# A four-layer Flamingo block on one core: two experts gated late, a third taken natively, and GpSimd work moved

## The chip, the cores and the metric

The kernel runs on one core of one Trainium2 chip. The metric is the device time in microseconds of one execution, lower is better. Five engines run side by side, each through its own list of instructions, and meet only at semaphores: TensorE (PE in the profile, its weight load PEld), VectorE (DVE), ScalarE (ACT), GpSimd (POOL) and SyncE (SP, which issues the DMAs).

## The reference

1024 tokens (4 batches of 256) of width 128 pass four residual layers, each behind a layer norm and scaled by the tanh of a scalar. Cut to what matters here:

```
x = x + tanh(gx0) * attention(LN(x), ctx)        # softmax(q k^T) v, 64 context rows per batch
x = x + tanh(gf0) * experts(LN(x))
x = x + tanh(gx1) * linear_attention(LN(x), ctx) # 16 heads of 8, softmax of q and k within a head
x = x + tanh(gf1) * quantised_mlp(LN(x))         # w_gate, w_up, w_down at 4 bits, width 384

def experts(tokens):                             # 8 experts, hidden 256
    top 2 of logits = tokens @ router_w.T;  gate[:, e] = softmax weight of expert e, or 0
    for e in range(8):
        h = gelu(tokens @ w1[e].T)
        out += gate[:, e:e+1] * (h @ w2[e].T)
```

The gate of an expert is one number per token, so it may be applied to the hidden values before the second product, or to the product itself.

## The kernel before

The tokens stand in two halves of 512 (HALVES, four tiles of 128 tokens each). The order on each engine is written out by hand.

**Experts.** The work of an expert is four units: half h (0, 1) by hidden chunk c (0, 1), so 32 units, u = 4e + 2h + c. A unit is: the product z on TensorE in three fp32r passes (high weights by high tokens, low by high, high by low), GELU on ScalarE out of PSUM (`gelu`), the gate times it on VectorE (`gate_unit`), and the second product y into bank 2 + h. For experts 2 to 6 that product is split as well: ScalarE rounds the gated values to a high part (`high`), VectorE takes the rest (`low`), and TensorE makes three passes. Experts 0, 1 and 7 are native: one fp32 product, which the trace shows as two instructions, and no `high` or `low`. A ring of NB = 4 banks and buffers holds the units in flight, and in the steady loop TensorE does y of unit u and then z of unit u + 4.

**Gates.** For each half `logits` gives the router's products, VectorE finds the best two (`top_two`) and the gates (`gates_of`). Expert 0 isn't gated before its second product: `y_first` writes bank h, and `first_expert` multiplies by the gate row late. Expert 1's row is spread over the partitions by TensorE (`second_gate`, eight small instructions a half) and copied by ScalarE. From expert 2 on the rows go through DRAM: `gate_columns` transposes, ScalarE copies to gateT, SyncE writes it to DRAM and reads it back spread over 128 partitions, expert by expert (512 KB), into q_exp and q_soft in turn.

**Beside it.** VectorE also prepares the 4-bit weights of the last layer (`weight_scales` after unit 7, `weight_rounds` after 12, `weight_values` after 15). TensorE transposes them (`weight_columns`, after units 22, 24 and 26), ScalarE copies them twice (after 23, 25 and 27), and GpSimd takes the difference wT_lo (L426) long after, in the attention that follows. The low halves of the expert weights are GpSimd's too (`low_weights`, L380).

**Start.** TensorE makes the tanh of the four scalars possible first, then keys, values, scores; `keep_warm` issues products of zeros. Then the second attention's keys and values (kv1) are computed in two calls of `context_rows`, which lie apart.

**After the experts.** `experts_to_tokens` transposes back, VectorE adds (`add_experts`), takes the statistics, and builds the queries (`q_values`, `q_less_max`). GpSimd computes the reciprocal deviations (`rstd_of`, L367), masks the key-value products (L418, L420), then takes wT_lo three times (L426), then q_soft (L432), which VectorE's L946 adds.

```
            rstd_of(5)
            rstd_of(6)
            ... masks of kv, then drain -> kv_ready
            for c in range(IC):          # wT_lo, L423 to L427
            for h in range(HALVES):      # q_soft, L428 to L434
```

## Time and profile before

| | |
|---|---|
| time, median of 3 runs | 153.59 us (150.95, 153.59, 156.99) |
| the profiled execution | 151.53 us, span 149.8 us, mean granted TensorE clock 0.943 |
| busy in the span | TensorE 82%, VectorE 81%, ScalarE 57%, GpSimd 21% |
| start and first attention | 0 to 22.3 us |
| gates and expert 0 | 22.3 to 39.1 us |
| the other experts | 39.1 to 81 us |
| second attention | 81 to 100 us |
| quantised layer | 100 to 149.8 us |

The span is the time from the first to the last instruction of the profiled execution. The stages were read off the order of the instructions.

### The profile page before, as it was taken

How to read it: one execution, taken by the hardware profiler on the slowest of the kernel's cores; microseconds unless marked ns; L12 is line 12 of the kernel's file. 1: busy time of each engine (PE TensorE's matmuls, PEld its weight loads, DVE VectorE, ACT ScalarE, POOL GpSimd, SP SyncE). 2: the span in 40 equal slices, each digit the busy share in tenths (PEclk: the TensorE clock that was granted, in tenths of full speed). 3: DMA queues.
4: the chain of work that ended last, by engine and by line, in shares of the span. 5: the costliest groups of instructions: out<-in, count | busy, mean ns of one | idle time of the engine just before them, and what ended most of it. 6: DMA issues, size and time to landing. Idle time of an engine off the chain costs nothing.

```text
span 149.8 us, 2084 instructions
## 1 busy us (share of the span) xinstructions
PE 122.4 (82%) x661; PEld 88.9 (59%) x661; DVE 121.7 (81%) x349; ACT 84.9 (57%) x149; POOL 30.9 (21%) x57
## 2 busy tenths in 40 slices
PE   6999979999899998999997958889999800019991
PEld 4586848785558876686663836668658500017860
DVE  4887778659699999987667897688478899899893
ACT  3244576585567787678771424152457697680570
POOL 1020321433970000000000499522010000000000
PEclk9999999999999999999999999999999995555899
DMA  4993000001183230411000000000000000000003
GB/s 137 328 415 154 7 0 0 0 0 40 43 260 155 77 135 8 140 75 69 0 0 0 0 0 2 4 2 0 0 0 4 0 2 0 0 0 0 0 0 140
DMA packets 3405, 8.23 MB, mean 55 GB/s; under 512 B 305, under 2 KB 1457, under 8 KB 3138
## 3 DMA queue, kind: packets, MB, share of 16 engines
q1 hardware_dynamic: 3392, 8.10, 14.7%
q8 instruction: 5, 0.08, 0.2%
q14 instruction: 6, 0.05, 0.1%
q10 hardware_dynamic: 2, 0.00, 0.0%
HBM read 7.54 MB, written 0.56 MB: 54 GB/s over the span
## 4 chain that ended last, share of the span: by engine, by line
PE 46%; DVE 25%; issue 11%; POOL 8%; ACT 7%; POOLq 1%; DVEq 0%; ACTq 0%
PE bank L1171 7%; PE bank L1167 6%; PE bank L1168 6%; PE bank L1144 5%; PE bank L1309 5%; DVE amax_u L1021 2%; PE bank L1295 2%; DVE amax_g L1021 2%; DVE hidden L1055 2%; DVE amax_p L1026 2%; POOL wT_lo L426 2%; DVE stats L648 2%; ACT wexp L615 2%; POOL rstd L367 2%; PE bank L1151 2%
## 5 line engine op out<-in xcount | busy, mean ns | idle before, releaser
L1144 PE MATMUL bank<-zero 128*128 128x256 f16 x177 | 28.5, 310 | 16.3 <-ACT ng L611 15.1
L1144 PEld LDWEIGHTS bank<-zero 128*128 128x128 f16 x177 | 18.7, 110 | 21.1 <-ACT ng L611 15.5
L508 ACT ACTIVATE hidden<-bank 128x512 f32<-128x512 f32 x32 | 18.8, 596 | 5.2 <-PE bank L1171 5.0
L367 POOL TENSOR_TENSOR rstd<-var,neg_half 128x4 f32<-128x4 f32 x6 | 6.1, 1018 | 53.5 <-DVE var L653 53.5
L857 DVE TENSOR_TENSOR low_parts<-hidden,high_parts 128x512 fp32r<-128x512 f32 x20 | 13.7, 684 | 3.0 <-ACT high_parts L514 3.0
L850 DVE TENSOR_TENSOR hidden<-hidden,q_soft 128x512 f32<-128x512 f32 x16 | 11.8, 744 | 4.1 <-ACT hidden L508 3.6
L514 ACT ACTIVATE high_parts<-hidden 128x512 fp32r<-128x512 f32 x20 | 12.6, 630 | 2.8 <-DVE hidden L850 2.5
L1167 PE MATMUL bank<-xhi,we_hi 128*128 128x512 f32 x28 | 13.6, 485 | 0.0
L380 POOL TENSOR_TENSOR we_lo<-wexp,we_hi 128x512 fp32r<-128x512 f32 (+1 forms) x8 | 9.5, 1209 | 11.1 <-DVE gate L784 6.9
L1171 PE MATMUL bank<-xlo,we_hi 128*128 128x512 f32 x28 | 11.1, 396 | 0.0
L1168 PE MATMUL bank<-xhi,we_lo 128*128 128x512 f32 x28 | 11.0, 394 | 0.0
L1171 PE MATMUL bank<-low_parts,we_hi 128*128 128x512 f32 x20 | 8.4, 420 | 0.6 <-DVE low_parts L857 0.4
L1167 PE MATMUL bank<-high_parts,we_hi 128*128 128x512 f32 x20 | 8.4, 421 | 0.2
L850 DVE TENSOR_TENSOR hidden<-hidden,q_exp 128x512 f32<-128x512 f32 x12 | 8.2, 680 | 0.5 <-ACT hidden L508 0.5
L1168 PE MATMUL bank<-high_parts,we_lo 128*128 128x512 f32 x20 | 7.9, 397 | 0.0
L1309 PE MATMUL bank<-hidden,wexp 128*128 128x512 f32 x16 | 7.8, 592 | 0.0
L615 ACT ACTIVATE wexp<-stream,mul_o 128x512 int16<-128x512 f32 x5 | 3.4, 710 | 5.9 <-DVE mul_o L998 5.9
L1168 PEld LDWEIGHTS bank<-xhi,we_lo 128*128 128x128 f32 x28 | 5.3, 188 | 2.3 <-issue 1.4
L1167 PEld LDWEIGHTS bank<-xhi,we_hi 128*128 128x128 f32 x28 | 5.3, 188 | 2.2 <-issue 1.4
L450 ACT ACTIVATE hidden<-bank 128x512 f32<-128x512 f32 x4 | 2.4, 598 | 6.6 <-PE bank L1429 5.1
L648 DVE BATCH_NORM_STATS2 stats<-stream 128x6 f32<-128x128 f32 x24 | 5.2, 279 | 1.0 <-DMA stream<-in_x 0.9
L1171 PEld LDWEIGHTS bank<-xlo,we_hi 128*128 128x128 f32 x28 | 5.3, 188 | 1.3
(255 smaller groups left out, 294.5 us busy)
## 6 DMA issues: line engine op xcount, KB each, us to landing
wexp<-in_experts SPq DMA_DIRECT2D x2, 1024.0 KB, 8.1
q_soft<-gates SPq DMA_DIRECT2D x3, 512.0 KB, 3.6
q_exp<-gates SPq DMA_DIRECT2D x2, 512.0 KB, 3.5
wq<-in_lpbq SPq DMA_DIRECT2D x1, 576.0 KB, 10.1
stream<-in_x SPq DMA_DIRECT2D x2, 256.0 KB, 3.6
q_exp<-gates SPq DMA_DIRECT2D x2, 256.0 KB, 3.2
xn<-gates SPq DMA_DIRECT2D x1, 512.0 KB, 5.1
out<-hidden SPq DMA_DIRECT2D x2, 256.0 KB, 2.0
```

The source lines that it names most:

```text
L367: pool.tensor_tensor(rstd[:, h, :], var[:, h, :], neg_half[:, :], ALU.pow).then_inc(rstd_ready, 1)
L380: pool.tensor_tensor(w_lo[e][:, cols], raw(e)[:, cols], w_hi[e][:, cols].bitcast(f32), ALU.subtract)\
L508: act.activation(ge[u % NB][:, :], bank[4 + u % NB][:, :], ACT.Gelu).then_inc(gelu_done, 1)
L514: act.activation(h_hi[u % NB][:, :], hm[u % NB][:, :], ACT.Copy).then_inc(hi_done, 1)
L648: m = step(dve.bn_stats(stats[:, h, t, :], src[:, h * TILES + t, :]))
L850: dve.tensor_tensor(hm[u % NB][:, :], ge[u % NB][:, :], half(gate_rows[e % 2], h), ALU.mult)\
L857: dve.tensor_tensor(h_lo[u % NB][:, :], hm[u % NB][:, :], h_hi[u % NB][:, :].bitcast(f32), ALU.subtract).then_inc(lo_done, 1)
L1144: mm(bank[b][:, 0:256], zero16[:, 0:128], zero16[:, 0:256], start=True, stop=True)
L1167: mm(dst, whi, xh, start=start, stop=False)
L1168: mm(dst, wlo, xh, start=False, stop=False)
L1171: return mm(dst, whi, xl, start=False, stop=stop)
L1309: last = mm(bank[2 + h][:, :], raw(e)[:, k], hm[u % NB][:, :], start=start, stop=stop)
```

## The change

**Experts.** Units are now addressed by their place p in ORDER (0, 1, 4, 5, 2, 3, 6, ...), so that experts 0 and 1 alternate by half. Both are ungated (LATE = 2): `y_first` serves eight units. ScalarE copies expert 0's result from bank h to y0 (`first_expert` there), then expert 1 takes the bank. VectorE gates y1 and y0 in `late_gate` and adds them in `late_sum`, six instructions of 128x512 in the split stretch (p = 13, 14, 16, 17, 19, 20). Expert 2 is native. `second_gate` is gone on TensorE and ScalarE. `logits` has passes of z between its tiles instead of `keep_warm`.

**Rows.** The gate rows come in halves of an expert (256 KB) into a ring of four; the rows of experts 0 and 1 (512 KB each) are read behind the fourth.

**Order.** ScalarE does GELUs, `high_weights` and copies in another order; the copy of the second attention's keys waits for both calls of `context_rows`. `top_two` is cut in `top_values` and `top_places`. `weight_scales` and `weight_rounds` go ahead of the second half's gates, `weight_values` to p = 11. `weight_columns` is issued after p = 17, 19, 21 on TensorE and copied after 20, 22, 24. GpSimd takes wT_lo before the masks, and the deviations 5 and 6 behind the masks of their k. The bias rows of the last projection and `key_products` are issued earlier, and some `keep_warm` counts change.

```
-        NATIVE = (0, 1, EXPERTS - 1)
-        Z_ORDER = [0, 1, 4, 5, 2, 3] + list(range(6, UNITS))
+        LATE = 2
+        GATED = LATE * FIRST
+        NATIVE = (0, 1, 2, EXPERTS - 1)
+        ORDER = [0, 1, 4, 5, 2, 3] + list(range(6, UNITS))
+        RING = 4
...
# SyncE
-            for e in range(3, EXPERTS):
-                sp.wait_ge(gated, (e - 2) * HALVES * FC)
-                sp.dma_start(gate_rows[e % 2][:, :], gates[e:e + 1, :].broadcast_to([128, TOKENS]))\
+            for k in range(HALVES, len(PAIRS)):
+                e, h = PAIRS[k]
+                if k >= RING:
+                    sp.wait_ge(gated, (k - RING + 1) * FC)
+                sp.dma_start(rows_at(k), half(gates, h)[e:e + 1, :].broadcast_to([128, HT]))\
+                    .then_inc(rows_in[k % RING], 16)
+                if k == RING - 1:
+                    for late in range(LATE):
+                        sp.dma_start(late_rows[late], gates[late:late + 1, :].broadcast_to([128, TOKENS]))\
...
# GpSimd
-            rstd_of(5)
-            rstd_of(6)
+            for c in range(IC):
+                low_columns(c)
             mask = head_mask[:, :, 0]
             for k in range(BPH):
...
+                rstd_of(5 + k)
             pool.drain().then_inc(kv_ready, 1)
-            for c in range(IC):
-                pool.wait_ge(wT_ready, c + 1)
...
# ScalarE, first attention
-            evac(k1[...], bank[2][:, 0:256], kv1_mm, 1, k1_ready)        # was ahead of exp_scores(0)
             exp_scores(0)
             prob_columns(0)
             evac(half(xT, 1), bank[7][:, :], xT_mm, 2, xT_ready)
-            for e in range(4):
+            for e in range(2):
                 high_weights(e)
+            evac(k1[...], bank[2][:, 0:256], kv1_mm, 2, k1_ready)
+            high_weights(2)
             evac(v1[...], bank[2][:, 256:512], kv1_mm, 2, k1_ready)
             exp_scores(1)
...
# VectorE
+            def late_gate(k, h):
+                dve.wait_ge(late_in[k], 16)
+                if k == 0:
+                    dve.wait_ge(y0_ready, h + 1)
+                    dve.tensor_tensor(half(y0, h), half(y0, h), half(late_rows[0], h), ALU.mult)...
+                else:
+                    dve.wait_ge(y_done, GATED)
+                    dve.tensor_tensor(half(y1, h), bank[h][:, :], half(late_rows[1], h), ALU.mult)...
+            gate_unit(GATED)
+            for p in range(GATED, UNITS):
+                if p + 1 < UNITS:
+                    gate_unit(p + 1)
+                if split(UNIT[p][0]):
+                    low(p)
+                if p == 11:
+                    weight_values()
+                elif p in (13, 14):
+                    late_gate(1, p - 13)
+                elif p in (16, 17):
+                    late_gate(0, p - 16)
+                elif p in (19, 20):
+                    late_sum(p - 19)
...
# TensorE
             pe.wait_ge(zero_ready, 1)
-            keep_warm(7, 9)
+            keep_warm(7, 19)
+            pe.wait_ge(pa_in, 16)
+            mm(bank[0][:, 0:256], A("wkT", D), A("ctxT", 256), start=True, stop=True).then_inc(kT_mm, 1)
...
             score_products(1)
+            context_rows(bank[2][:, 0:256], B("wkT"), R("bk1")).then_inc(kv1_mm, 1)
             context_rows(bank[2][:, 256:512], B("wvT"), R("bv1")).then_inc(kv1_mm, 1)
...
-            logits(0)
+            pe.wait_ge(pv_read, HALVES)
+            logits(0, (2, 3))
             y_first(0)
             y_first(1)
-            z_unit(4)
-            z_unit(5)
             normalised(bank[1], 4)
-            second_gate(0)
-            first_pair(1)
-            logits(1)
-            gate_columns(0)
             y_first(2)
             y_first(3)
-            z_unit(6)
-            second_gate(1)
+            gate_columns(0)
+            first_pair(4)
+            logits(1, (6, 7))
+            y_first(4)
+            y_first(5)
+            z_unit(8)
             gate_columns(1)
-            z_unit(7)
+            z_unit(9)
+            y_first(6)
+            y_first(7)
+            z_unit(10)
+            z_unit(11)
...
-            experts_to_tokens(1)
+            key_products(0)
             pe.wait_ge(x3_ready, 1)
             transposes(bank[6], x3, 0).then_inc(xT_mm, 1)
-            key_products()
+            experts_to_tokens(1)
+            key_products(1)
```

## Rows read from the trace of the kernel before

**Rows 1.** Busy time by stage: stretch, its length, each engine's busy us, granted clock, DMA

```profile
22.30:39.10 16.80, 16.00 (x97) 12.21 (x95) 12.69 (x66) 10.75 (x22) 6.60 (x6) 1.00 0.05 18
45.20:66.00 20.80, 20.24 (x86) 15.49 (x85) 20.70 (x33) 15.67 (x28) 0.00 (x0) 1.00 0.24 87
66.00:81.00 15.00, 14.84 (x60) 9.19 (x59) 9.65 (x15) 10.51 (x21) 0.00 (x0) 1.00 0.09 36
81.00:91.00 10.00, 6.74 (x56) 5.72 (x56) 9.29 (x32) 2.98 (x7) 6.34 (x12) 1.00 0.00 0
112.00:150.00 38.00, 19.53 (x93) 14.14 (x91) 32.95 (x63) 22.50 (x29) 1.43 (x4) 0.78 0.04 14
```

**Rows 2.** GpSimd in order of time: start, length, operation, idle time before it

```profile
85.49 1.01 POOL L367 TENSOR_TENSOR rstd<-var,neg_half 128x4 f32<-128x4 f32 x1 [1.17 <-DVE var L653]
...
89.42 3.36 POOL L426 TENSOR_TENSOR wT_lo<-wT,wT_hi 128x384 fp32r<-128x384 f32 x3 [0.18 <-issue]
92.75 1.49 POOL L432 TENSOR_TENSOR q_soft<-q_exp,inv 128x128 f32<-128x128 f32 x4
```

**Rows 3.** VectorE in order of time: start, length, operation, idle time before it

```profile
11.82 0.42 DVE L717 TENSOR_TENSOR sc<-bank,smax 128x256 f32<-128x256 f32 x1
...
37.97 1.30 DVE L850 TENSOR_TENSOR hidden<-hidden,q_soft 128x512 f32<-128x512 f32 x1 [0.38 <-ACT q_soft L526]
...
46.32 0.68 DVE L850 TENSOR_TENSOR hidden<-hidden,q_exp 128x512 f32<-128x512 f32 x1
...
50.14 1.35 DVE L705 TENSOR_TENSOR ng<-wq,wb_r 128x1152 int16<-128x1152 f32 x1
...
94.34 0.69 DVE L946 TENSOR_TENSOR hidden<-hidden,q_soft 128x512 f32<-128x512 f32 x1 [1.30 <-POOL q_soft L432]
```

**Rows 4.** ScalarE in order of time, first attention and weight columns

```profile
12.63 0.38 ACT L450 ACTIVATE k<-bank 128x256 f32<-128x256 f32 x1 [2.25 <-PE bank L1183]
12.91 0.41 ACT L482 ACTIVATE sc<-sc 128x256 f32<-128x256 f32 x1
...
17.86 0.39 ACT L450 ACTIVATE v<-bank 128x256 f32<-128x256 f32 x1 [1.26 <-PE bank L1183]
19.40 0.42 ACT L482 ACTIVATE sc<-sc 128x256 f32<-128x256 f32 x1 [1.16 <-DVE sc L717]
...
71.94 0.49 ACT L532 ACTIVATE wT_hi<-bank 128x384 fp32r<-128x384 f32 x1 [0.84 <-PE bank L1320]
```

**Rows 5.** TensorE in order of time, first attention

```profile
3.79 2.10 PE L1144 MATMUL bank<-zero 128*128 128x256 f16 x9
...
8.33 0.71 PE L1144 MATMUL bank<-zero 128*128 128x256 f16 x5
...
11.26 0.69 PE L1181 MATMUL bank<-row,ones 1*128 1x256 f32 x2
11.88 0.71 PE L1183 MATMUL bank<-pb,pa 128*128 128x128 f32 x4
...
16.48 0.69 PE L1181 MATMUL bank<-row,ones 1*128 1x256 f32 x2
```

**Rows 6.** Chain of work that ended last, gate stage: start, length, what

```profile
24.20 0.26 PE bank L1144 x2
...
29.32 0.89 PE bank L1342 x8
...
32.34 0.15 PE bank L1144
...
36.11 1.14 PE bank L1342 x8
...
38.77 0.24 PE bank L1168
39.00 0.23 PE bank L1171
39.23 0.86 PE bank L1309 x2
```

**Rows 7.** TensorE in order of time, gate stage's end and split stretch

```profile
37.92 0.60 PE L1333 MATMUL bank<-ident,gate 128*8 128x128 f32 x4 [0.69 <-ACT q_soft L526]
...
57.63 0.51 PE L1171 MATMUL bank<-low_parts,we_hi 128*128 128x512 f32 x1 [0.42 <-DVE low_parts L857]
```

**Rows 8.** Waits of TensorE's weight load, 55 to 81 us: total, times, longest

```profile
PEld bank L1171 <- DVE low_parts L857: 2.5, 5, 0.9
PEld bank L1167 <- ACT high_parts L514: 1.0, 2, 0.5
```

**Rows 9.** DMA issues by line: queue, count, KB each, median us to landing

```profile
xn<-gates SPq DMA_DIRECT2D x1, 512.0 KB, 5.1
```

**Rows 10.** Busy time by stretch, the transfers of the gate rows: last columns DMA share, GB/s

```profile
43.00:45.00 2.00, 2.00 (x8) 1.29 (x7) 1.93 (x5) 1.47 (x3) 0.96 (x3) 1.00 1.02 393
```

**Rows 11.** Costliest groups of GpSimd: count, busy us, mean ns

```profile
L418 POOL TENSOR_TENSOR kv<-kv_raw,head_mask 128x128 f32<-128x128 f32 x4 | 2.2, 539 | 0.0
...
L420 POOL TENSOR_TENSOR kv<-kv_raw,head_mask 128x16 f32<-128x16 f32 x4 | 0.9, 220 | 0.0
```

More of the change, by code:

```diff
@@ L765, in top_two, with top_places @@
                 dve.tensor_tensor(g2_[:, h, :], best[:, :, 1], best[:, :, 0], ALU.subtract).then_inc(dm_ready, 1)
+            def top_places(h):
+                lg, best, place, top1, top2, gate = router_tiles(h)
+                order = number[:, :].unsqueeze(1).broadcast_to(wide_gates)
+                dve.wait_ge(number_ready, 1)
                 for t in range(TILES):
@@ L1256, in _, with z_passes, z_unit, logits @@
             keep_warm(1, 4)
-            def logits(h):
+            def z_passes(p, which):
+                e, h, c = UNIT[p]
+                out_ = bank[4 + p % NB][:, :]
+                k = slice(c * D, (c + 1) * D)
+                for n in which:
+                    if n == 0:
+                        pe.wait_ge(xhi_ready, h + 1)
+                        pe.wait_ge(we_split, e + 1)
+                        if p >= NB:
+                            pe.wait_ge(gelu_done, p - NB + 1)
+                        mm(out_, w_hi[e][:, k], half(xhi, h), start=True, stop=False)
+                    elif n == 1:
+                        mm(out_, w_lo[e][:, k], half(xhi, h), start=False, stop=False)
+                    else:
+                        pe.wait_ge(xlo_ready, h + 1)
+                        mm(out_, w_hi[e][:, k], half(xlo, h), start=False, stop=True).then_inc(z_ready, 1)
+            def z_unit(p):
+                z_passes(p, (0, 1, 2))
+            def logits(h, beside):
                 pe.wait_ge(xlo_ready, h + 1)
@@ L1310, in y_unit @@
+                    last = three(bank[2 + h][:, :], w_hi[e][:, k], w_lo[e][:, k], h_hi[p % NB][:, :],
+                                 h_lo[p % NB][:, :], start, stop, (lo_done, split_count(p)))
+                else:
+                    pe.wait_ge(gated, p - GATED + 1)
+                    last = mm(bank[2 + h][:, :], raw(e)[:, k], hm[p % NB][:, :], start=start, stop=stop)
                 last.then_inc(y_done, 1)
@@ L1404, in _ @@
                 last.then_inc(q_mm, 1)
-            keep_warm(5, 8)
+            pe.wait_ge(kv_raw_ready, BPH)
+            for k in range(HALVES):
+                bias_rows(bank[2 + k], 1)
+            keep_warm(5, 4)
             for h in range(HALVES):
@@ L1410, in _ @@
                 last.then_inc(qeT_mm, 1)
-                if h == 0:
-                    keep_warm(7, 3)
-                else:
-                    pe.wait_ge(kv_raw_ready, BPH)
-                    for k in range(HALVES):
-                        bias_rows(bank[2 + k], 1)
+                keep_warm(5 if h == 0 else 7, 3)
                 pe.wait_ge(kv_ready, 1)
```

328 lines of the change are left out of this document (145 added, 183 removed).

## Prediction

> **What bounds the kernel now.** I read the busy time by stage first, then the chain of work that ended last, then each engine's order of time around the edits. In the gate stage and the expert stages TensorE is busy 16.00 of 16.80, 20.24 of 20.80 and 14.84 of 15.00 us at a granted clock of 1.00: whatever TensorE is spared there comes off the end, unless a wait takes its place [rows 1]. VectorE is nearly as full in the middle one, 20.70 of 20.80 us, which makes it the first candidate for a new bound; in the next it has 9.65 of 15.00. In the second attention the load changes: TensorE 6.74 of 10 us, VectorE 9.29, and on GpSimd three subtractions of 3.36 us stand directly before the q_soft products, which VectorE then waits for, 1.30 us the first time [rows 1, 2, 3]. The quantised layer, the last 38 us, isn't touched.
>
> **Start, 0 to 22.3 us.** Before the first softmax ScalarE waited 2.25 us for the key product kv1, copied it, and only then took the exponential, at 12.91 us [rows 4]. That copy moves behind. The scores and their subtraction were ready some 0.6 us earlier (VectorE's last step began at 11.82 and took 0.42) [rows 3], so the first half gains 0.6 to 0.9 us; the longer keep_warm run of 19 with the scalar product moved behind it takes TensorE to the same place as before within 0.2 us. But both kv1 calls now follow score_products(1). One is 1.2 to 1.3 us, a bias pair and four products [rows 5]. TensorE reaches them about 0.8 us sooner than it reached the second one (16.48), at 15.7, and needs 2.5 us: 18.2. Behind that end ScalarE has the key copy, a high_weights and the value copy (0.38 + 0.4 + 0.3 us), then the second exponential, at 19.35 us against 19.40 [rows 4]. So most of the gain is taken back by this wait: what is queued behind the waiting copy is the softmax of half 1, and behind it the normalisation whose transposes start the experts. What is left is the normalisation itself, then 0.35 us earlier, since its deviations come from the first half. I take -0.35, bounds 0 and -0.9 (all of the first half's gain).
>
> The tanh of the scalars moves from first place to behind the first token copy. It is 0.2 us in 2 us of ScalarE's idle time and costs nothing.
>
> **Gate stage, up to the second product of unit 8.** Work removed from TensorE: second_gate, 0.89 + 1.14 us, and the keep_warm instructions between the logits, three pairs of 0.26 and three single ones whose 0.15 is mostly the router product's own time, some 0.04 of it their own: 0.9 us [rows 6]. Idle time removed: before gate_columns(1) TensorE waited 0.69 us for the copy of second_gate, which no longer exists [rows 7]. New there: expert 1 may take bank 0 only when ScalarE has copied expert 0's result. The copy is 0.6 us and the transposes between (0.44) hide most of it: 0.15 us of waiting; for bank 1 a z unit, the columns and another z cover it. gate_columns(1) waits for the second half's gates. By my order of time the logits end at 35.0 (2.5 us with the z passes between), the two-best search and the gates take VectorE until 37.5, and TensorE arrives at 37.8 after two y_first and a z: 0.3 us of cover. VectorE itself must be rid of the key softmax, weight_scales (1.9) and weight_rounds (1.3) [rows 3] by then; from 30.1 it ends at about 34.9, just in time. Sum: -2.03 - 0.9 - 0.7 + 0.15 + 0.25 for the thin cover = -3.2 us. Bounds -3.5 and -1.8 (VectorE 1.4 us late, as much as one weight step).
>
> **Expert 2 native.** A split product is three passes of 0.235 us, 0.70; a native one is 0.86 [rows 6]. Four units: +0.65 us on TensorE, which is the bound. The four high and four low that go (0.6 us each) free engines that are not the bound at p = 8 to 11.
>
> **The split stretch.** A unit there is 1.40 us of TensorE and, on VectorE, a gate and a low at 0.60 us from start to start. So it has 0.2 us a unit to spare, 3.2 over 16 units; it must carry six late instructions, 3.6 us, after weight_values of 1.3. Before, the same stretch carried weight_rounds, weight_values and two gatings, 3.8 us, and the weight load waited 2.5 us in five pieces for low parts and 1.0 us in two for high parts, of which some 1.7 us were real gaps between products, by their starts in TensorE's order of time, the largest 0.42 [rows 7, 8]. About 1.0 of those stand around the three weight_columns, where ScalarE waited for transposes that TensorE had not reached [rows 4]. Now the transposes are issued three units ahead of their copies, so these go. Of the rest I keep 0.6, since VectorE, laid out instruction by instruction, comes within 0.2 us of each third pass from p = 14 to 20. Term: -1.7 + 0.6 = -1.1 us, bounds -1.7 and +1.5. Two things could use up that margin. **Rows:** the three row halves and the two late rows are 1.8 MB at once where 1.3 MB went before; the last of these took 5.1 us to land [rows 9]. With 0.5 MB more, at the rate of the fullest stretch (393 GB/s) [rows 10], the row of expert 1 lands at about 48 us, and late_gate(1, 0) is reached at 48.6 to 50. It is issued last though wanted first, and a late landing holds the gates and lows behind it on VectorE. **GpSimd:** a gate took 1.30 us beside a GpSimd subtraction and 0.68 us alone [rows 3]; the expert weights' low halves now reach to about 48 us, beside weight_values, and the wT_lo subtractions fall at 60 to 67 us. Three of them at up to 0.6 us each lengthen VectorE by 1.8 us at most, just after the last late_sum, where it gains 0.2 us a unit. I count 0.2 of the 0.6 for them.
>
> The Trainium skill ("SBUF — State Buffer", section "SBUF: two separate sides") speaks against this move: GpSimd and a VectorE instruction with two SBUF inputs take one port pair in turn, and the loser blocks for the other's whole instruction. The doubled gate agrees. By the rule alone each subtraction of about 1.1 us would be added whole to VectorE, and the term would be worse by another 1.5 us, the first rival below.
>
> **After the experts.** The 3.36 us of wT_lo leave this stage [rows 2]. What is late next: kv_ready. GpSimd now does the masks of k = 0, deviation 5, masks of k = 1, deviation 6; the masks sum to 2.8 us or less [rows 11], the deviations to 2.0, and starting 1.0 us after the last expert product it ends at +5.7 us against +8.3 before. Deviation 5 still ends at +3.3 and is wanted at +4.6, deviation 6 at +5.6 against +7.1: covered. VectorE is then the bound to the queries, and gains 0.2 us from the earlier query product and 0.2 from the missing neighbour. The reciprocals begin at about 90.9 instead of 91.2 (all times here as if the experts had ended at 81.0), GpSimd's four q_soft need 1.5 us behind them with 0.5 in parallel, and L946 stands at 92.9 instead of 94.34 [rows 3]. For the second half the bias products no longer stand before the value products, the reciprocals follow at 93.6, q_soft again lies on the path for 1.5 us, and L946 comes at 95.75 instead of 97.19. So not 3.36 but 1.4 us, bounds -0.5 (the queries or kv_ready hold it) and -1.8.
>
> **Sum.** -0.35 - 3.2 + 0.65 - 1.1 - 1.4 = -5.4 us: span 149.8 to 144.4, and the profiled execution's own 151.53 to 146.1. The three runs shown scatter from 150.95 to 156.99 with their median 2.06 above the profiled one; by the median the same sum gives 148.2. I predict 147.0, between the two. A measurement of this kernel can tell about 2% (3 us) from no change.
>
> **Rivals.**
> 1. *VectorE becomes the bound of the expert stage* (chance 0.17). For: 20.70 of 20.80 us busy, the doubled gate, the late row issued last. Against: 2.4 us less VectorE work over the experts (four lows and four gates of 0.6 go and so do two late gatings, six late instructions come), and room in the next stretch. It costs 3 us of the sum: 150.
> 2. *TensorE stands at gate_columns(1)*, its in-order list waiting for gates that the weight steps delayed, or at the start for the second softmax (0.13). For: the cover is 0.3 us. Against: the two weight steps end just when the logits do. 1.5 us: 148.5.
> 3. *The GpSimd move gives nothing*, because the queries end the wait (0.05). 1.4 us, 148.4. Against: the 1.30 us wait.
> 4. *Slower: TensorE's clock rises later* (0.05). It stood at the 1.2 GHz level in the first products (nine in 2.10 us) and at the 2.4 GHz level at 8.33 us (0.11 us apart) [rows 5]. The change swaps real products for zeros ahead of the rise and thins them behind. If the higher level came only with the experts, some 8 us of TensorE's list in the start would be added and all else late: 155. It decides from 5.4 us lost, so from 11 us of dense list at the lower level. Against: the list stays as full as before; the granted clock held 1.00 even through the 10 us at 67% busy.
>
> **How the numbers follow.** Forecast 0.6 (144 to 149). Range 143.8 to 151.5: the lower end is the best bounds of the start, gates and attention without the median's excess, the upper takes in rivals 1 to 3 with it. Faster by over 2% means under 150.5: the forecast, rivals 2 and 3 mostly, and part of rival 1: 0.80. Within 2%: 0.14. Slower 0.06, rival 4 and the scatter of the runs.
>
> **What would show it.** The first y of unit 8 at about 42.2 us, the last expert product at 77 us (81.0 before), the second exponential near 19.35, no wait of ScalarE for transposes of weights, GpSimd idle before q_soft and L946 within 0.3 us of it, 0.6 us or less of waits for low parts. Wrong if a gate stands at late_in, if gate_columns(1) shows idle time of TensorE over 0.5 us, or if the stage from 81 on is not shorter by 1 us.

## The result, and the profile after

The changed kernel takes 149.67 us (149.33 to 151.96, 20 runs) against 151.44 us (150.74 to 156.99, 20 runs), a ratio of 0.9905 [0.9883, 0.9927]. The times are medians of all runs, and the ratio leaves out the slow executions of both kernels, so it isn't quite the ratio of the two times. The gain is real, 1.0 to 1.2%, but small: the sum promised 3.6% of the span, and I had named 147.0 us. The profiled execution took 149.6 us, with a span of 147.8 against 149.8 before: 2.0 us gained, 5.4 forecast.

Busy time by stage of the changed kernel, cut at the first z product, the first product of unit 8, the last expert product and the last q_soft sum (columns as in [rows 1]):

```profile
21.95:42.16 20.21, 19.73 (x89) 13.32 (x89) 14.23 (x69) 12.27 (x25) 5.65 (x5) 1.00 0.08 20
42.16:79.96 37.80, 35.84 (x141) 23.66 (x139) 33.72 (x47) 25.75 (x48) 15.30 (x12) 1.00 0.31 102
79.96:95.18 15.22, 12.55 (x87) 10.13 (x88) 13.26 (x45) 5.02 (x9) 7.31 (x18) 1.00 0.00 1
95.18:147.80 52.62, 32.55 (x194) 23.62 (x192) 43.91 (x102) 29.17 (x41) 3.93 (x7) 0.87 0.03 11
```

The same four marks stood at 22.58, 45.47, 81.06 and 97.19 before, and the second stage, that of the experts from unit 8 on, was:

```profile
45.47:81.06 35.59, 34.85 (x143) 24.45 (x142) 30.08 (x47) 26.12 (x48) 0.00 (x0) 1.00 0.17 63
```

So the change was 0.63 us ahead at the first mark, 3.31 at the second, only 1.10 at the third, and 2.01 at the fourth. The second stage gives 2.2 us back. It holds 15.30 us of GpSimd work, where the same stage of before held none, and VectorE is busy 33.72 us in it, where it was 30.08.

The 0.63 us at the first mark are not the change's. Here is one product of the start, first in the kernel before, then in experiment 10 below, which has the same start:

```profile
5.68 1.06 PE L1229 MATMUL bank<-pa 128*128 128x256 f32 x2
```

```profile
5.57 0.60 PE L1229 MATMUL bank<-pa 128*128 128x256 f32 x2
```

In the profiled execution of the kernel before TensorE ran longer at its lower clock, and everything behind it came some 0.6 us later. The first z product stands at 22.33 there, but at 21.72, 21.79 and 21.82 in experiments 10, 11 and 4, which start as the kernel before does. The changed kernel has it at 21.70. (These are the starts in TensorE's order of time; the chain that ended last, from which the four marks are taken, puts this one 0.25 later.) Against such an execution the change gains 1.2 to 1.4 us of span: the changed kernel with more zeros (experiment 7) has a span of 148.0, the kernel before with more zeros (experiment 10) 149.2.

TensorE in order of time, changed kernel, three places:

```profile
28.96 1.96 PE L1328 MATMUL bank<-hidden,wexp 128*128 128x512 f32 x4 [0.34 <-ACT y L466]
...
37.74 0.60 PE L1367 MATMUL bank<-ident,gate 128*8 128x128 f32 x4
...
70.55 0.50 PE L1198 MATMUL bank<-low_parts,we_hi 128*128 128x512 f32 x1 [1.17 <-DVE low_parts L880]
```

The first is the new wait of expert 1 for bank 0. The second is gate_columns(1), where TensorE stood 0.69 us in [rows 7] and now doesn't stand. The third is the largest hole of the split stretch. By a hole I mean the time by which the start of a product comes later than the usual spacing after the product before it. From unit 8 on TensorE lost 0.24, 0.55, 0.18, 0.30, 0.30, 0.20 and 1.33 us in this way, 3.1 in all, against 1.7 before with 0.59 as the largest.

The chain that ended last has the first product of unit 8, the second mark, here:

```profile
42.16 0.86 PE bank L1342 x2
```

VectorE in order of time, changed kernel:

```profile
43.76 2.59 DVE L874 TENSOR_TENSOR hidden<-hidden,q_exp 128x512 f32<-128x512 f32 x2 [3.00 <-DMA q_exp<-gates]
...
46.89 1.37 DVE L727 TENSOR_TENSOR wb_i<-ng,wb_s 128x1152 f32<-128x1152 int16 x1
...
49.44 0.88 DVE L874 TENSOR_TENSOR hidden<-hidden,q_soft 128x512 f32<-128x512 f32 x1
50.24 0.94 DVE L880 TENSOR_TENSOR low_parts<-hidden,high_parts 128x512 fp32r<-128x512 f32 x1
51.11 0.68 DVE L890 TENSOR_TENSOR x4T<-bank,x 128x512 f32<-128x512 f32 x1
...
65.55 0.68 DVE L874 TENSOR_TENSOR hidden<-hidden,q_exp 128x512 f32<-128x512 f32 x1
66.28 1.38 DVE L880 TENSOR_TENSOR low_parts<-hidden,high_parts 128x512 fp32r<-128x512 f32 x1
67.58 1.50 DVE L874 TENSOR_TENSOR hidden<-hidden,q_exp 128x512 f32<-128x512 f32 x1
69.01 1.49 DVE L880 TENSOR_TENSOR low_parts<-hidden,high_parts 128x512 fp32r<-128x512 f32 x1
70.42 0.68 DVE L874 TENSOR_TENSOR hidden<-hidden,q_exp 128x512 f32<-128x512 f32 x1
...
90.10 1.10 DVE L955 RECIPROCAL inv<-bank 128x64 f32<-128x64 f32 x2 [0.49 <-PE bank L1447]
...
92.34 0.69 DVE L973 TENSOR_TENSOR hidden<-hidden,q_soft 128x512 f32<-128x512 f32 x1 [0.40 <-POOL q_soft L448]
...
95.18 0.69 DVE L973 TENSOR_TENSOR hidden<-hidden,q_soft 128x512 f32<-128x512 f32 x1 [0.54 <-POOL q_soft L448]
```

And GpSimd in order of time:

```profile
43.39 2.41 POOL L394 TENSOR_TENSOR we_lo<-wexp,we_hi 128x512 fp32r<-128x512 f32 x2 [1.47 <-ACT we_hi L482]
45.76 3.20 POOL L415 TENSOR_TENSOR kv<-head_mask 128x16 f32<-128x16 f32 x4
...
62.34 6.20 POOL L427 TENSOR_TENSOR wT_lo<-wT,wT_hi 128x384 fp32r<-128x384 f32 x2 [10.84 <-ACT wT L548]
68.87 1.08 POOL L427 TENSOR_TENSOR wT_lo<-wT,wT_hi 128x384 fp32r<-128x384 f32 x1 [0.33 <-ACT wT L548]
...
90.74 1.50 POOL L448 TENSOR_TENSOR q_soft<-q_exp,inv 128x128 f32<-128x128 f32 x4 [5.23 <-DVE inv L955]
```

The three pieces of wT_lo alone (shortest, median and longest in ns, then first and last start):

```profile
L427 POOL TENSOR_TENSOR wT_lo<-wT,wT_hi x3: 1077/1471/4774, 62.3 to 68.9; 128x384 fp32r<-128x384 f32 x3
```

Lay the two engines beside each other. From 46.3 to 74 us VectorE has no wait longer than 0.05 us: a 128x512 step starts every 0.60 us where nothing lengthens it, the shortest spacing in either kernel. The two gates that started at 43.76 ran beside the low halves of the expert weights and took 2.59 us, not 1.3. Two steps at 49.44 ran beside three one-partition instructions. From 66.28 three steps took 1.4 to 1.5 us each. They ran beside wT_lo, whose three pieces took 4.77, 1.47 and 1.08 us, where all three had taken 3.36 [rows 2]. The first piece is on record from 62.34 on, yet the six VectorE steps that start beside it up to 65.55 keep their 0.68 us. Only the next, which starts 0.73 us and not 0.60 after the one before, takes 1.38, and then the piece ends. So while VectorE's steps follow each other without a gap it is GpSimd that stands, and once GpSimd gets in each piece lengthens one step. TensorE's 1.33 us hole at 70.55 is the end of the three. The late step at 51.11 has no wait before it: the gate row that I feared would land late was there.

### The profile page after: what moved, and what is told of

Same layout as the page of the kernel before. It is cut to its first block, busy times and chain, and to the rows that moved or that the text cites. A ratio compares the mean times of both kernels' runs of the same rounds, so it can differ in the third digit from the quotient of the medians.

```text
span 147.8 us, 2032 instructions
## 1 busy us (share of the span) xinstructions
PE 120.3 (81%) x630; PEld 85.1 (58%) x630; DVE 121.9 (82%) x345; ACT 81.8 (55%) x145; POOL 36.5 (25%) x57
## 4 chain that ended last, share of the span: by engine, by line
PE 40%; DVE 30%; issue 15%; ACT 10%; POOL 3%; POOLq 0%; DVEq 0%; ACTq 0%
PE bank L1171 5%; PE bank L1328 5%; DVE low_parts L880 4%; DVE hidden L874 4%; PE bank L1342 4%; PE bank L1294 3%; PE bank L1299 3%; PE bank L1296 3%; DVE amax_u L1048 2%; DVE amax_g L1048 2%; DVE hidden L1082 2%; DVE amax_p L1053 2%; ACT wexp L632 2%; PE bank L1178 2%; POOL q_soft L448 2%
## 5 line engine op out<-in xcount | busy, mean ns | idle before, releaser
L1171 PE MATMUL bank<-zero 128*128 128x256 f16 x166 | 25.1, 302 | 17.1 <-ACT ng L628 15.1
L524 ACT ACTIVATE hidden<-bank 128x512 f32<-128x512 f32 x32 | 18.5, 591 | 8.9 <-PE bank L1299 8.6
L1294 PE MATMUL bank<-xhi,we_hi 128*128 128x512 f32 x32 | 15.7, 490 | 0.0
L874 DVE TENSOR_TENSOR hidden<-hidden,q_exp 128x512 f32<-128x512 f32 x12 | 10.1, 857 | 4.9 <-DMA q_exp<-gates 3.0
L530 ACT ACTIVATE high_parts<-hidden 128x512 fp32r<-128x512 f32 x16 | 10.2, 634 | 7.0 <-DVE hidden L874 6.9
L394 POOL TENSOR_TENSOR we_lo<-wexp,we_hi 128x256 fp32r<-128x256 f32 (+1 forms) x8 | 8.5, 1075 | 15.9 <-DVE gate L806 9.9
L427 POOL TENSOR_TENSOR wT_lo<-wT,wT_hi 128x384 fp32r<-128x384 f32 x3 | 7.3, 2441 | 11.2 <-ACT wT L548 11.2
L874 DVE TENSOR_TENSOR hidden<-hidden,q_soft 128x512 f32<-128x512 f32 x12 | 8.4, 701 | 1.2 <-ACT hidden L524 1.2
L1342 PE MATMUL bank<-hidden,wexp 128*128 128x512 f32 x16 | 7.9, 597 | 0.1
L1328 PE MATMUL bank<-hidden,wexp 128*128 128x512 f32 x16 | 7.6, 596 | 0.3 <-ACT y L466 0.3
L1194 PE MATMUL bank<-high_parts,we_hi 128*128 128x512 f32 x16 | 6.6, 414 | 0.0
```

The costliest lines, as they stand in the source:

```text
L394: pool.tensor_tensor(w_lo[e][:, cols], raw(e)[:, cols], w_hi[e][:, cols].bitcast(f32), ALU.subtract)\
L427: pool.tensor_tensor(wT_lo[:, k, :], wT[:, k, :], wT_hi[:, k, :].bitcast(f32), ALU.subtract)\
L524: act.activation(ge[p % NB][:, :], bank[4 + p % NB][:, :], ACT.Gelu).then_inc(gelu_done, 1)
L530: act.activation(h_hi[p % NB][:, :], hm[p % NB][:, :], ACT.Copy).then_inc(hi_done, 1)
L874: dve.tensor_tensor(hm[p % NB][:, :], ge[p % NB][:, :], rows_at(k), ALU.mult).then_inc(gated, 1)
L1171: mm(bank[b][:, 0:256], zero16[:, 0:128], zero16[:, 0:256], start=True, stop=True)
```

## The experiments

Each is timed against the kernel before; "warm" marks a kernel with more keep_warm instructions (zeros for TensorE) around the attention, twelve in those from the changed kernel. Where a stretch is named, "last product" is the end of the last expert product and "attention" the time from there to the second q_soft sum.

**1. wT_lo back behind kv_ready, all else of the change kept.**

```diff
-            for c in range(IC):
-                low_columns(c)
             mask = ...
             pool.drain().then_inc(kv_ready, 1)
+            for c in range(IC):
+                low_columns(c)
```

> The changed kernel with one part undone: GpSimd's three wT_lo subtractions stand behind the masks, the deviations and kv_ready again, where GpSimd was idle for 5.2 us before q_soft. Theory (in the expert stretch VectorE is the bound, and these subtractions lengthened three of its instructions from 0.68 to 1.4 to 1.5 us, with 1.3 us of gap in TensorE behind the last): the last expert product comes 1.3 to 2.2 us earlier, at 77.8 to 78.7 us instead of 79.96; the subtractions fit in the 5.2 us, so L973 stays 12.4 us behind it; 1.2 to 2.2 us faster than the changed kernel's 149.67, so 147.5 to 148.4. Rival 1 (the gain of the attention came from the move of wT_lo itself): the attention loses its 0.9 us again, 148.5 to 149.4 in all. Rival 2 (the gap before 70.55 is something else's, a row or ScalarE): no change of the expert stretch, 149.7 to 150.5.

Measured: 149.1 us (148.45 to 149.34), ratio 0.9833 [0.9799, 0.9868], span 147.4. The 1.33 us hole is gone and the last product ends at 78.34 instead of 79.96, 1.62 us earlier. But the total moved by 0.6. Stretches of the attention, columns as in [rows 1]:

```profile
84.00:86.00 2.00, 1.43 (x8) 0.68 (x6) 1.93 (x5) 0.33 (x1) 1.91 (x2) 1.00 0.01 4
86.00:88.00 2.00, 1.50 (x8) 0.93 (x8) 1.93 (x5) 0.90 (x2) 1.45 (x2) 0.67 0.00 0
88.00:90.00 2.00, 2.00 (x8) 2.00 (x9) 0.68 (x2) 0.63 (x1) 0.00 (x0) 0.50 0.00 0
90.00:92.00 2.00, 1.55 (x12) 1.28 (x12) 1.40 (x6) 0.60 (x1) 1.54 (x4) 0.97 0.00 0
```

The granted clock falls from 1.00 to 0.50, the 1.2 GHz level, after stretches in which TensorE stood idle in pieces of 0.63 and 0.93 us, and VectorE waits for slow products:

```profile
89.41 0.56 DVE L954 RECIPROCAL inv<-bank 128x64 f32<-128x64 f32 x1 [1.29 <-PE bank L1446]
```

The rule that TensorE's clock starts throttled and is released by activity is in the Trainium skill ("TensorE: Matmul & The Clock Gate", section "Part 1: The HAM clock gate"). The traces agree as to the direction: in the start nine products took 2.10 us at 3.79 and five 0.71 us at 8.33, with TensorE at work between [rows 5], and the 0.50 above comes after idle pieces. The changed kernel's own profile held 1.00 through the same stage. Twelve of its 20 runs took 149.3 to 149.8 us, the other eight 150.3 to 151.96.

**2. Six late instructions over 8 columns.** late_gate and late_sum of both halves are cut to `[:, 0:8]`; this leaves out the gating of experts 0 and 1 in the other columns.

> The changed kernel with the six late instructions of VectorE (four late_gate, two late_sum) over 8 of their 512 columns: the gating of experts 0 and 1 is left out for the other columns. All waits and signals stay. It prices these six. Theory (VectorE is the bound from 45 to 74 us): six times some 0.5 us go from VectorE, and TensorE gets back its gaps of 0.2 to 0.55 us between 49 and 56, and part of the last one because VectorE comes into the wT_lo subtractions with more lead: 1.5 to 2.7 us faster than 149.67. Rival (TensorE is the bound and the six lie beside it, as the prediction had it, with gaps of 0.6): 0.6 us at most.

Measured: 147.35 us (147.16 to 148.4), ratio 0.9747 [0.971, 0.9785], last product at 77.74. In VectorE's order of time a late step is

```profile
51.25 0.15 DVE L890 TENSOR_TENSOR x4T<-bank,x 128x8 f32<-128x8 f32 x1
```

and takes 0.08 us from start to start where the full one takes 0.60. The 1.33 us hole shrinks to 0.23 although wT_lo still runs there. VectorE now has gaps, wT_lo's pieces take 1.01, 1.13 and 1.26 us, and the three steps beside them 1.09, 1.20 and 1.33 instead of 1.38 to 1.50. So the six instructions and wT_lo draw on one reserve: either alone nearly fits, both don't, and a VectorE list without gaps makes the collision dearer for both engines. They cost the whole kernel 2.3 us (149.67 - 147.35) of the 3.1 that the cut saves VectorE (six by 0.52).

**3. weight_values at place p = 8 instead of 11.**

```diff
-                if p == 11:
+                if p == 8:
                     weight_values()
```

> The changed kernel with weight_values (1.37 us on VectorE) moved from p = 11 to p = 8, where VectorE sits idle for 3.0 us until the row of the second half has landed. Theory (VectorE is the bound behind that point): the instruction disappears in the idle time, VectorE enters the split stretch 1.3 us earlier, the gaps of TensorE at 49.6, 51.2, 53.0 and 54.9 us (1.3 us together) go, and the last one shrinks: 1.0 to 1.6 us faster than 149.67. Rival (the gaps come from the landing of the rows, which this leaves alone): 0.3 us or less.

Measured: 149.59 us (148.71 to 149.9), ratio 0.987 [0.9831, 0.9909]. The step now fills the time in which VectorE waited for the second half's first gate row. It lasts longer there, beside GpSimd:

```profile
40.56 2.45 DVE L727 TENSOR_TENSOR wb_i<-ng,wb_s 128x1152 f32<-128x1152 int16 x1
```

Of the four holes between 49 and 56 us one is left, 0.30, but the last one stays at 1.34: TensorE gets there 1.26 us earlier as well, so VectorE has no more lead over it than before. The last product ends at 78.70, 1.26 us earlier, and nothing of it reaches the end. The granted clock is 0.50 in the window from 88 to 90 us. By this run alone it can't be said that the clock takes it; runs 5 to 7 ask that.

**4. The kernel before, with wT_lo moved early and nothing else.**

```diff
             pool.drain().then_inc(const_late, 1)
+            for c in range(IC):
+                pool.wait_ge(wT_ready, c + 1)
+                ...  # wT_lo, moved here from behind kv_ready
```

> The kernel before with the wT_lo move alone: GpSimd takes the three subtractions as soon as the weights are transposed, about 69 to 77 us, ahead of the deviations 5 and 6; nothing else changed. There VectorE has idle time between its instructions (9.65 busy of 15 us). Theory (the move costs where VectorE is full and gains where it isn't): L946 no longer waits 1.30 us for q_soft in the attention, -1.0 to -1.4 us; in the expert stretch the last units lose 0 to 0.7 us; 0.3 to 1.4 us faster than before. Rival (something else holds the attention at once): within 0.3 us of before.

Measured: 151.87 us (150.74 to 155.48), ratio 1.0017 [0.9987, 1.0048], again with a clock of 0.50 in the attention (92 to 94 us). It doesn't separate the theories until the clock is held: experiment 11 does that.

**5. to 7. Twelve more keep_warm instructions**: experiment 5 (f1 in the text below) is experiment 3 with them, 6 (f2) is experiment 1 with them, 7 (f3) is the change as it is with them.

```diff
             key_products(1)
+            keep_warm(1, 5)
             pe.wait_ge(x3_ready, HALVES)
...
-            keep_warm(5, 4)
+            keep_warm(5, 11)
```

> e4_values_early plus twelve more keep_warm instructions in TensorE's idle time of the attention: five ahead of the second half's transposes of x3, seven more ahead of the query transposes. In e4_values_early the last expert product came 1.3 us earlier than in the changed kernel, but the granted clock was 0.50 from 88 to 90 us and the value products took 2.47 us instead of 1.32, so the total did not move. Theory (the fall of TensorE's clock in the attention hid the gain, and it falls because TensorE idles there): the clock stays at 1.00 up to 112 us and the gain shows, 148.2 to 148.6, about 1.1 us under e4_values_early. Rival (the fall has nothing to do with idle time there): the granted clock falls again, 149.3 to 149.9.

> e1_wtlo_back plus the same twelve keep_warm instructions. In e1_wtlo_back the last expert product came at 78.34 us, 1.62 us earlier than in the changed kernel, and the value products took 2.37 us at a granted clock of 0.50. Theory: without the fall the attention is as long as in the changed kernel, since the wT_lo subtractions end at 87.5 us, before q_soft can start: 147.7 to 148.2. Rival (part of the longer attention in e1_wtlo_back is the subtractions beside VectorE's query work): 148.4 to 148.9 with the clock at 1.00.

> The changed kernel plus the twelve keep_warm instructions and nothing else. Of its 20 runs, those with a mean clock of 0.954 have a span of 147.8 us, those with 0.93 to 0.943 one of 148.9 to 149.3. Theory (the clock falls in some of its executions and costs about 1.1 us there): the low ones stay at 149.5, the high ones go, so the median falls by 0 to 0.3 us and the highest by 1 us. Rival (the added products get in the way of the transposes): 149.9 or more.

Measured: f1 148.59 (148.34 to 148.91), ratio 0.9816 [0.9793, 0.9839]; f2 148.23 (148.0 to 148.39), 0.9787 [0.9763, 0.9811], at the edge of what was expected; f3 149.73 (149.67 to 150.0), 0.9894 [0.9872, 0.9916]. In f1 the clock is 1.00 in the windows where experiment 3 had 0.50:

```profile
86.00:88.00 2.00, 1.69 (x14) 1.07 (x11) 1.93 (x7) 1.20 (x2) 0.00 (x0) 1.00 0.01 4
88.00:90.00 2.00, 1.83 (x15) 1.81 (x15) 1.51 (x3) 0.69 (x3) 0.37 (x2) 1.00 0.00 0
```

With the zeros the two single edits give 1.0 and 0.9 us more than without (149.59 to 148.59, 149.10 to 148.23). The changed kernel itself keeps its median, and none of its six runs lies above 150.0. Against f3, weight_values early is worth 1.1 us and wT_lo back 1.5. And f2 shows something else. Its VectorE in the attention, last product at 78.63:

```profile
88.92 1.10 DVE L954 RECIPROCAL inv<-bank 128x64 f32<-128x64 f32 x2 [0.49 <-PE bank L1447]
...
94.01 0.69 DVE L972 TENSOR_TENSOR hidden<-hidden,q_soft 128x512 f32<-128x512 f32 x1 [0.54 <-POOL q_soft L447]
```

The attention takes 15.38 us, against 15.25 in f3. GpSimd does wT_lo at 84.39 to 87.76 and still waits 1.80 us before q_soft. So in the changed kernel the early wT_lo brings nothing (0.13 us) there. In f2 GpSimd starts the masks 1.2 us after the last expert product and in the kernel before 5.4 us after it, behind both deviations. By its order of time that is enough to free q_soft; but this move was not undone by itself, so the cause is argued and not shown.

**8. All cheap moves together, warm**: wT_lo back, weight_values at p = 8, and GpSimd's small masks and bias rows between the low halves of experts 4, 5 and 6.

> The version the runs point to: the changed kernel with wT_lo back behind kv_ready, weight_values at p = 8, GpSimd's kv masks and bias rows (L415 to L420) put between the expert weights' low halves where VectorE idles, and the twelve keep_warm instructions. Theory (VectorE is the bound of the split stretch, and GpSimd beside it lengthens it): the steps hardly overlap until TensorE is the bound, with a floor of 34.4 us from the first product of unit 8; TensorE's gaps of 3.1 us shrink to 0.5, so 2.5 us off: 146.8 to 147.4. Rival (another wait, ScalarE's or the rows', takes their place): 148 or more.

Measured: 147.78 us (147.64 to 147.98), ratio 0.9763 [0.9739, 0.9787], 0.4 us short of what was expected. The gains don't quite add (1.1 + 1.5 against 1.95). Part of that is the start: in this profile the granted clock is 0.50 from 17.6 to 21.0 us, and the first z product comes at 22.17 instead of 21.80. From there to the last expert product it is 2.4 us shorter than f3. And one hole is new, 0.54 us at 47.67. VectorE, then GpSimd:

```profile
44.07 3.54 DVE L875 TENSOR_TENSOR hidden<-hidden,q_exp 128x512 f32<-128x512 f32 x2 [0.47 <-DMA q_exp<-gates]
```

```profile
45.10 1.96 POOL L394 TENSOR_TENSOR we_lo<-wexp,we_hi 128x512 fp32r<-128x512 f32 x2
```

Two gates of 1.3 us became 3.54 beside the low halves that the small steps had pushed back. The two took 0.75 and 2.87 us: the second starts ahead of both low halves, 0.35 us ahead of the first, and ends behind both. Here moving GpSimd work did not take away its collision, it picked the VectorE step that pays.

**9. Expert 2 split again, warm.** `NATIVE = (0, 1, EXPERTS - 1)`.

> f3_after_warm (149.73) with expert 2 split again, as before the change: one name out of NATIVE, so four units get their high and low parts and three passes instead of one fp32 product. It prices that part of the change. Theory (VectorE is the bound from 44 us on): four more lows at 0.6 us on VectorE come ahead of the split stretch, where it has no idle time left, against 0.65 us less on TensorE and a longer low half of expert 2 on GpSimd in its idle time: 1.2 to 2.4 us slower, 150.9 to 152.1. Rival (TensorE's own products set the pace, as the prediction's term had it): 0.65 us faster, 149.1.

Measured: 152.43 us (152.34 to 152.74), ratio 1.0077 [1.0055, 1.01]: 2.7 us slower than f3, and 0.8% slower than the kernel before. TensorE at the first split unit, then VectorE, then ScalarE:

```profile
44.42 0.47 PE L1194 MATMUL bank<-high_parts,we_hi 128*128 128x512 f32 x1 [2.12 <-ACT high_parts L530]
```

```profile
39.62 1.29 DVE L874 TENSOR_TENSOR hidden<-hidden,q_exp 128x512 f32<-128x512 f32 x2 [1.88 <-ACT hidden L524]
44.31 1.05 DVE L880 TENSOR_TENSOR low_parts<-hidden,high_parts 128x512 fp32r<-128x512 f32 x1 [3.40 <-ACT high_parts L530]
```

```profile
41.65 1.29 ACT L524 ACTIVATE hidden<-bank 128x512 f32<-128x512 f32 x2 [1.05 <-PE bank L1299]
42.84 0.93 ACT L482 ACTIVATE we_hi<-wexp 128x512 fp32r<-128x512 f32 x2
43.66 1.14 ACT L530 ACTIVATE high_parts<-hidden 128x512 fp32r<-128x512 f32 x2
```

The gated values of units 8 and 9 are ready at 40.91. Their high parts start at 43.66 all the same, since ScalarE's list has the GELUs of units 10 and 11, for which it waits 1.05 us, and two high_weights ahead of them. That order suited a native expert 2, and the edit left it as it is. It gives TensorE a hole of 2.27 us. A second one, 1.37 us at 52.87, stands behind weight_values, which took 1.61 us beside GpSimd, and a gate of 0.94. Both are larger than the 0.65 us that the native products cost TensorE. So the run shows that the change, ordered as it is, needs expert 2 native. It isn't the price of four more low parts, which was the theory, and how a split expert 2 would do with its high parts further ahead was not tried.

**10. and 11. The kernel before, warm, without and with wT_lo early.** Fifteen more zeros: `keep_warm(1, 3)` in the same place, `keep_warm(5, 8)` made `(5, 20)`.

> The kernel before with more keep_warm in the attention: three ahead of the second half's transposes of x3, twenty instead of eight ahead of the query transposes, where TensorE idled 1.64 us. A control for the clock. Theory: the fast executions of before held the clock, so 151.2 to 151.6, within 0.3 us of before. Rival (before loses time to the clock too): 0.5 us or more faster.

> g2_before_warm with the wT_lo subtractions moved into the expert stretch (e5_before_wtlo_early with the keep_warm): the move alone, with the clock held. In e5_before_wtlo_early the clock stood at 0.50 from 92 to 94 us. Theory (the move takes 3.4 us off GpSimd in the attention and q_soft then waits only for the reciprocals): L946 comes 0.9 us earlier against the last expert product, and the expert stretch loses 0.4 to 0.8 us (two lows of 1.09 instead of 0.69 us): 0.1 to 0.5 us faster than g2_before_warm. Rival (no loss in the expert stretch, as at the end of the prediction's list): 0.9 us or more faster.

Measured: 151.04 (150.8 to 153.58), ratio 0.9977 [0.9953, 1.0], and 151.3 (150.84 to 153.43), ratio 0.9995 [0.9961, 1.0028]. Between the two stands the moved wT_lo: the last product goes from 80.4 to 81.3, the attention from 16.1 to 15.2 us. VectorE of the second:

```profile
91.46 1.10 DVE L928 RECIPROCAL inv<-bank 128x64 f32<-128x64 f32 x2 [0.49 <-PE bank L1422]
...
93.69 0.69 DVE L946 TENSOR_TENSOR hidden<-hidden,q_soft 128x512 f32<-128x512 f32 x1 [0.40 <-POOL q_soft L432]
...
96.54 0.69 DVE L946 TENSOR_TENSOR hidden<-hidden,q_soft 128x512 f32<-128x512 f32 x1 [0.40 <-POOL q_soft L432]
```

Here, unlike in the changed kernel, the move does gain in the attention, 0.9 us, as the wait before the first sum is 0.40 us and not 1.30 [rows 3]. The expert stage takes it back. There VectorE has gaps, and the collision is cheap for GpSimd, whose three pieces take 1.01 us each, while three VectorE steps take 1.08 to 1.10 instead of 0.68:

```profile
69.08 1.08 DVE L857 TENSOR_TENSOR low_parts<-hidden,high_parts 128x512 fp32r<-128x512 f32 x1 [1.02 <-ACT high_parts L514]
```

The warm before also shows that the zeros alone are worth 0.4 us at most, with an interval that touches no change. In the two profiles its lead of 0.66 us of span is 0.61 at the first z product already, far ahead of the zeros.

**12. Experiment 8 with the last four high halves earlier on ScalarE.** high_weights(4) and (5) behind (3); (6) and (7) behind gate_columns(0).

> f4_all_warm with ScalarE's high_weights 4 to 7 moved ahead into its idle time at 29.8 to 32.5 and 34.5 to 36 us, so that GpSimd takes all low halves from 38 us on without waiting. In f4_all_warm two gates took 3.54 us beside GpSimd's low halves 6 and 7 and TensorE waited 0.54 us at 47.7. Theory (that wait goes with its neighbour): 0.3 to 0.6 us faster, 147.2 to 147.5. Rival (the same subtractions now stand beside the gates of units 8 and 9, and gate_tanh behind two high_weights delays the gates): no change or 0.5 us slower.

Measured: 147.47 us (147.37 to 147.78), ratio 0.9747 [0.9724, 0.9771], span 145.6. It is the fastest version that leaves nothing out, 1.5% below the changed kernel. Its median is 0.3 us under that of experiment 8, but not by the reason given: the hole at the same product is there, 0.58 us at 47.29. From the first z product to the last expert product the two profiles take the same time, 55.90 and 55.85 us. The difference between them is the start, 21.74 against 22.17, where the clock of experiment 8 had fallen. That the edit gained anything is not shown.

## Why the prediction was wrong

The failed step is one term, "-1.7 + 0.6 = -1.1 us, bounds -1.7 and +1.5", the split stretch. Its holes went from 1.7 to 3.1 us, so it came to +1.4, at the far bound. With it came the first rival, "VectorE becomes the bound of the expert stage", priced at 150; 149.67 was measured. That the price fits so well is partly luck: it started from 147.0, which holds half of a 2.06 us excess of three runs, and with 20 runs the median of before lies within 0.1 us of its profiled execution.

- **Start.** Forecast -0.35, measured -0.63 against the profiled execution of before, but -0.02 to -0.12 against three executions with the same start and an earlier clock (21.72, 21.79 and 21.82, here 21.70). So the 0.35 did not come, and the 0.63 is the luck of one profile. The first exponential is 0.30 us earlier than in experiment 10 (11.99 against 12.29), where 0.6 to 0.9 was forecast; the second is 0.31 later (19.09 against 18.78). The wait that takes the gain back is there (ScalarE, for the key product, until 18.24), and it takes all of it.
- **Gate stage.** Forecast -3.2, measured -2.7 (3.31 less 0.63). The first product of unit 8 stands at 42.16, forecast 42.2, since the 0.63 of the start makes up for it. The missing half lies mainly in the keep_warm instructions between the logits, priced at 0.9. By the starts of TensorE's products, and with the six passes of z taken at 0.235 each, the first half's logits went from 1.71 to 1.41 us and the second half's from 1.39 to 1.33: 0.36 in all. Ahead of the first of them TensorE now also pauses for 0.3 us, where the new wait for pv_read stands (VectorE reads that bank until 23.2). The wait for bank 0 was 0.34 instead of 0.15, and the 0.25 us allowed for gate_columns(1) was not needed. No run took these apart. Rival 2 is out.
- **Expert 2.** TensorE's own cost of 0.65 us is right. I priced it on TensorE alone and said that the freed VectorE and ScalarE time was worth nothing "at p = 8 to 11". Undoing it costs 2.7 us in the changed order, and the largest new hole there, 2.27 us, is a wait of TensorE for ScalarE. So the freed time was worth something there, but how much of it a better order would save is not shown.
- **Split stretch.** Right: the holes around weight_columns went (no 0.24 and 0.16 pairs any more), and no gate stood at late_in. Wrong: the reserve. I put it at 0.2 us a unit over 16 units, 3.2 us, and named the claims on it, but netted them one by one. Against rival 1 I set "2.4 us less VectorE work over the experts"; from unit 8 on VectorE's busy time in fact rose by 3.6 us (30.08 to 33.72), partly since the four gates of expert 1 that went had stood ahead of unit 8, partly since steps beside GpSimd grew. The six late steps (3.6 us) alone overdraw the reserve; weight_values (1.3), the contention of the low halves, the small steps and wT_lo all fall in the same stretch, and most of each microsecond more becomes TensorE's idle time (2.3 of 3.1 in experiment 2). I "count 0.2 of the 0.6 for them" (wT_lo); taking it out gave 1.5 us (f2 against f3), and narrowing the late steps 2.3.
- **The rule on the port.** Beside the three pieces of wT_lo VectorE's steps took 1.38, 1.50 and 1.49 us instead of 0.68, and the first piece took 4.77 beside six steps of 0.68 and one of 1.38. The prediction weighed the Trainium skill's rule ("SBUF — State Buffer", section "SBUF: two separate sides") against 0.2 us. By it one of the two engines blocks for the other's whole instruction. An estimate by it and the shortest piece of 1.08 us is 1.76 for such a step: the direction agrees, the size is 0.3 to 0.4 us smaller each. The first piece goes beyond it: it stood through six of VectorE's steps and not through one. For the whole kernel the prediction took 1.5 us more from the rule, and 1.5 was measured (f2 against f3). The rule was the better guide here than the margin that I set against it, but the equal number is luck in part: the prediction doesn't show how three pieces of 1.1 us make 1.5.
- **Attention.** Forecast -1.4, measured -0.9. The failed part is the first reciprocal: 10.14 us after the last product, 10.15 before, where 0.3 less was forecast. TensorE's in-order list has the second half's transposes ahead of the first query products, and VectorE's statistics come last before them; the chain that ended last goes that way. The mechanism was also told wrongly: in this kernel all but 0.13 us of the gain is there without wT_lo's move (15.38 us with wT_lo back), most likely by the earlier masks and drain. In the kernel before, wT_lo's move gives it too. Rival 3, that the GpSimd move gives nothing, is nearly true of wT_lo in the changed kernel, and its cost is not a gain missed but 1.5 us lost among the experts.
- **Clock.** Rival 4 did not come: at 5.82 us five products of zeros took 0.71 us, the faster spacing that [rows 5] show at 8.33, and the granted clock is 1.00 from there to the end of the experts. A clock that falls later, in the attention, I had not priced. It took 0.9 to 1.0 us of experiments 1 and 3. It may explain the upper runs of the changed kernel: with the zeros none of six lies above 150.0, where eight of 20 had. But none of those eight was profiled, and experiment 8 shows that the clock can also fall in the start.

Sum by its terms: the forecast end of 144.4 missed by 3.4 us, 0.24 up to unit 8, 2.66 in the expert stage, 0.49 in the attention. Of the 2.66, 1.4 + 1.1 are holes (3.1 against the forecast 0.6) and 0.16 are unaccounted for. With the start counted as it is in experiments 4, 10 and 11 the miss is 0.6 larger. The range had a slip as well: the best bounds that it names for its lower end add up to 144.9 and not to 143.8.

What stays open is why TensorE's clock falls in some executions and not in others. In the attention of experiments 1, 3 and 4 it was busy between 0.75 and 2.00 us of each 2 us from 78 us up to the fall. In the changed kernel's profile it was busy 1.21 to 2.00, without a fall. In the start of experiment 8 it was busy for all of the 2 us ahead of 18.

## What to carry to other kernels

When several steps are moved into one engine's gaps, add all of them up against that engine's reserve over the stretch, at the length they have beside GpSimd, before any is called hidden, and count each step in the stretch where it stands, not over the whole kernel. Price a swap of a fast form for a slow one on every engine that feeds it, not only on the one that runs it. When one move of a hand-laid order is undone, see which wait took its place before calling the difference its price. Before a gain in an early stage is believed, hold it against other executions of the same code: one profile of before was 0.6 us late by its clock alone. When an edit that plainly shortens a stage does not shorten the total, look at the granted clock of the next stage before giving the edit up.

## What the runs showed of the hardware

- **Both engines lose, and most when VectorE has no gaps.** wT_lo's three pieces took 4.77, 1.47 and 1.08 us beside a VectorE list without gaps, 1.1 each in [rows 2], and lengthened three VectorE steps by 0.7 to 0.8 each. Where VectorE had gaps (experiment 11) they took 1.01 each and lengthened three steps by 0.4. Four steps of 128x16 on GpSimd (`kv<-head_mask`) took 0.66, 0.66, 1.33 and 0.66 us beside two-input steps of VectorE, the longest beside weight_values; in the kernel before they took 0.71 and three times 0.21.
- **Small steps collide too, for less.** One-partition steps of 128 elements on GpSimd took 0.78 to 0.90 us, 0.39 to 0.46 before, and stretched two 128x512 steps from 0.68 to 0.88 and 0.94. The large ones cost 0.7 to 0.8.
- **The half clock shows on short products.** The eight key-value products of the first half took 2.37 us in experiment 1 at a granted clock of 0.50 and 1.32 in experiment 5 at 1.00. With twelve zeros in TensorE's own idle time the clock is 1.00 in every stretch of 2 us from 78 to 92 us in the profiles of experiments 5, 6, 8 and 12, and none of their 21 timed runs lies over 0.4 us above its median.
